# Gated cross-attention with a mixture of experts on one core: the turned selection goes to GpSimd, the low half of the second weights to VectorE, the additions take the high halves first, and the result is formed by bank and stored by tile

## The reference

```python
e = idx.reshape(-1)
onehot = jax.nn.one_hot(e, E, dtype=jnp.int32)
pos = jnp.sum(onehot * (jnp.cumsum(onehot, axis=0) - 1), axis=1)
valid = pos < CAP
buf = jnp.zeros((E, CAP, D), xt.dtype).at[e, posc].add(x_pairs)
g = jnp.einsum('ecd,eid->eci', buf, W1)
u = jnp.einsum('ecd,eid->eci', buf, W3)
h = jax.nn.silu(g) * u
out = jnp.einsum('eci,edi->ecd', h, W2)
y_pairs = out[e, posc] * (w.reshape(-1) * valid)[:, None]
...
x = x + jnp.tanh(g_ffn[0]) * (y + shared)
```

## Time and profile before

| what | value |
|---|---|
| median of 3 runs | 411.07 us (410.23 to 413.1) |
| span of the profiled execution, first to last instruction | 405.0 us |
| median of the runs less that span | 6.07 us |
| PE busy | 358.6 us, 89% |
| DVE busy | 303.5 us, 75% |
| ACT busy | 250.9 us, 62% |
| POOL busy | 124.1 us, 31% |
| the expert loop (start of the first pass's first weights to the last addition) | 333.6 to 399.7 us |

### The profile page before, as it was taken

One profiled execution on the slowest core, in us unless ns is written; L12 is line 12 of the kernel. 1 busy time (PEld: TensorE's weight loads), 2 busy tenths in 40 slices (PEclk: granted clock), 3 DMA queues, 4 the chain that ended last, 5 costly groups with the idle time before them and its releaser, 6 DMA issues.

```text
span 405.0 us, 14019 instructions
## 1 busy us (share of the span) xinstructions
PE 358.6 (89%) x5793; PEld 269.3 (67%) x5793; DVE 303.5 (75%) x656; ACT 250.9 (62%) x412; POOL 124.1 (31%) x116
## 2 busy tenths in 40 slices
PE   0896899999998998998999999998864699999993
PEld 0663468668677766855866776786643587888882
DVE  3888886775776676586577668668896877999993
ACT  3476477777686676776768666567721535666761
POOL 6151462132022122222203300001101054787870
PEclk9999699999999999999999999999985858999998
DMA  7869965565294186166336208544000009635001
GB/s 253 196 157 197 241 146 134 87 159 136 58 171 115 53 152 182 54 106 175 103 61 125 54 14 142 129 137 141 3 2 2 1 1 306 191 116 163 2 0 45
DMA packets 34512, 45.65 MB, mean 113 GB/s; under 512 B 3995, under 2 KB 30299, under 8 KB 34323
## 3 DMA queue, kind: packets, MB, share of 16 engines
q1 hardware_dynamic: 33395, 43.74, 44.5%
q0 software_dynamic: 640, 0.78, 0.9%
q10 hardware_dynamic: 416, 0.26, 0.3%
HBM read 25.08 MB, written 0.47 MB: 63 GB/s over the span
## 4 chain that ended last, share of the span: by engine, by line
PE 76%; DVE 13%; issue 5%; ACT 2%; POOL 2%; DMA 1%; DVEq 0%; ACTq 0%; POOLq 0%
PE PS L1035 35%; PE PS L1101 9%; PE PS L1078 8%; PE PS L1112 7%; PE PS L1363 4%; PE PS L1322 3%; DVE mx L794 2%; PE PS L1088 2%; PE PS L1346 2%; PE PS L1312 1%; DMA x_in<-x 1%; DVE KN L743 1%; PE PS L1279 1%; DVE st L697 1%; DVE mtop L798 1%
## 5 line engine op out<-in xcount | busy, mean ns | idle before, releaser
L794 DVE TENSOR_REDUCE mx<-PS 112x1 f32<-112x500 f32 (+1 forms) x128 | 114.3, 933 | 52.8 <-PE PS L1078 52.7
L501 ACT ACTIVATE PT_all<-PS 128x1344 f32<-128x1344 f32 x64 | 82.6, 1290 | 10.1 <-PE PS L1101 9.9
L1035 PE MATMUL PS<-cT,wkvT 128*128 128x500 f16 x288 | 71.5, 385 | 18.0 <-POOL slot_of L404 11.2
L1035 PE MATMUL PS<-wkvT,cT 128*125 128x256 f16 x576 | 73.2, 279 | 0.0
L1035 PEld LDWEIGHTS PS<-wkvT,cT 128*125 128x125 f16 x576 | 65.3, 139 | 5.3 <-issue 0.5
L395 POOL TENSOR_TENSOR cT<-c_in,cT 128x1000 f16<-128x1000 f32 x18 | 37.5, 2082 | 86.9 <-ACT cT L479 86.9
L1035 PEld LDWEIGHTS PS<-cT,wkvT 128*128 128x128 f16 x288 | 27.5, 99 | 50.8 <-POOL slot_of L404 11.2
L486 ACT ACTIVATE KN<-PS,col_in 128x500 f16<-128x500 f32 x48 | 32.5, 677 | 40.6 <-PE PS L1035 40.6
L1078 PE MATMUL PS<-arena,QC 96*112 96x500 f16 x192 | 52.4, 380 | 3.1 <-issue 2.8
L1101 PE MATMUL PS<-QC,arena 98*128 98x112 f16 x768 | 49.2, 214 | 3.0 <-ACT QC L521 2.9
L493 ACT ACTIVATE V<-PS 125x512 f32<-125x512 f32 x48 | 28.7, 598 | 30.6 <-PE PS L1035 30.6
(11 more groups left out here) (207 smaller groups left out, 463.8 us busy)
## 6 DMA issues: line engine op xcount, KB each, us to landing
arena<-KN SPq DMA_DIRECT2D x144, 125.0 KB, 3.6
c_in<-ctx SPq DMA_DIRECT2D x24, 500.0 KB, 4.5
cT<-W SPq DMA_DIRECT2D x11, 352.0 KB
c_in<-W SPq DMA_DIRECT2D x6, 352.0 KB
cT<-W SPq DMA_DIRECT2D x11, 176.0 KB
arena<-place_far SPq DMA_DIRECT2D x1, 1568.0 KB, 10.0
c_in<-W SPq DMA_DIRECT2D x6, 176.0 KB
PT_all<-L_xattn_wkv SPq DMA_DIRECT2D x1, 512.0 KB, 6.1
```

Source lines behind the costliest of these rows:

```text
L501: act.activation(PT_all[:, u % 4, :].rearrange("p (c k) -> p c k", c=CH), PS[:, 3:6, 0:4 * TP], ACT.Exp, scale=SCORE).then_inc(s["exp_done ...
L794: dve.tensor_reduce(mx[:, u % 2, k:k + 1], PS[0:TP, k:1 + k * (CH - 1), 0:CW], AX.XY, ALU.max).then_inc(s["red_done"], 1)
L1035: ins = mm(out_, w(a, h), x_(b, h), start=first and k == 0, stop=last and k == len(todo) - 1)
```

## The change

Four edits, all in the expert loop and behind it.

1. `turned_select` moves from VectorE to GpSimd. It is the same instruction, issued there in a plain loop over the experts. Its waits are the same: the transfer of the places for experts 0 and 2, and `added` for the buffer.
2. `w2_lo` moves from GpSimd to VectorE for the experts 1 to 16 (index 0, the shared expert, stays). On VectorE it is one instruction that scales and subtracts, straight from the loaded weights, so the scaling step goes. It stands where the turned selection stood.
3. `add` runs over the high half for all four tiles first, and waits for the low half only then. In the last `add` a semaphore is raised after the second and the fourth tile.
4. The result is formed bank by bank after that semaphore, and each tile is stored by a transfer of its own.

```diff
+            out_v = out.rearrange("b s d -> (b s) d").rearrange("(t p) d -> p t d", p=TP)
+            for t in range(TT):
+                sp.wait_ge(s["y_final"], t + 1)
+                sp.dma_start(out_v[:, t, :], y_out[:, t, :]).then_inc(s["stored"], 16)
+            sp.wait_ge(s["stored"], 16 * TT)
...
-            for j in range(1, E + 1):
-                need(gp, "w2l_done", j)
-                w2_lo(j)
+
+            def turned_select(e):
+
+                if e == 0:
+                    gp.wait_ge(s["place_in0"], 16)
+                elif e == 2:
+                    gp.wait_ge(s["place_in1"], 16)
+                need(gp, "added", e - 1)
+                gp.tensor_scalar(selT[e % 2], place_row[:, e, :], slot_of[:, 0:1], None, ALU.is_equal).then_inc(s["st_done"], 1)
+
+            for e in range(E):
+                turned_select(e)
...
+            def w2_lo(j):
+
+                need(dve, "w2h_done", j + 1)
+                need(dve, "w2l_done", j)
+                dve.scalar_tensor_tensor(w2T[j % 2][:, 1], w2_in[j % NW], FS, w2T[j % 2][:, 0], ALU.mult, ALU.subtract).then_inc(s["w2l_done"], 1)
...
-                turned_select(e)
                 if e + 1 < E:
+                    w2_lo(e + 2)
                     hidden_rows(e + 1)
...
             w13_lo(1)
+            w2_lo(1)
...
             def add(e):
 
-                need(pe, "yl_done", e + 1)
                 need(pe, "st_done", e + 1)
-                for t in range(TT):
-                    for a in range(2):
+                for a in range(2):
+                    need(pe, "yl_done" if a else "yh_done", e + 1)
+                    for t in range(TT):
                         last = mm(PS[0:TP, t // 2, (t % 2) * D:(t % 2 + 1) * D], selT[e % 2][:, t * TP:(t + 1) * TP], y16[:, a, :],
                                   start=False, stop=e == E - 1 and a == 1, skip_group_check=True)
-                last.then_inc(s["added"], 1)
+                        if e == E - 1 and a == 1 and t % 2 == 1:
+                            last.then_inc(s["bank_added"], 1)
+                if e < E - 1:
+                    last.then_inc(s["added"], 1)
```

More of the change, by code:

```diff
@@ L254, in program @@
             gu_ready tanh_done h_done ht_ready hh_done hl_done y_ready yh_done yl_done added
-            y_final stored""".split()
+            bank_added y_final stored""".split()
         s = {n: sem(n) for n in names}
@@ L355, in _ @@
                 load_weights(j)
-            sp.wait_ge(s["y_final"], 1)
-            sp.dma_start(out.rearrange("b s d -> (b s) d").rearrange("(t p) d -> p t d", p=TP), y_out[:]).then_inc(s["stored"], 16)
-            sp.wait_ge(s["stored"], 16)
+            out_v = out.rearrange("b s d -> (b s) d").rearrange("(t p) d -> p t d", p=TP)
[3 more added lines that the diff above has]
+            sp.wait_ge(s["stored"], 16 * TT)
         @block.gpsimd
@@ L442, in _ @@
                         context_lo(b + 2, c)
[L443 to L449, removed]
-            need(gp, "t_ready", SLOTS - NPAIR)
-            w2_lo(0)
+            need(gp, "t_ready", SLOTS - NPAIR)
+            gp.wait_ge(w_in[0], 32)
+            gp.tensor_scalar(w2_s, w2_in[0], FS, None, ALU.mult).then_inc(s["w2_scaled"], 1)
+            gp.wait_ge(s["w2_scaled"], 1)
+            gp.wait_ge(s["w2h_done"], 1)
+            gp.tensor_tensor(w2T[0][:, 1], w2_s, w2T[0][:, 0], ALU.subtract).then_inc(s["w2l_done"], 1)
             for k, part in enumerate(groups):
@@ L1019, in _ @@
             result_lo(E - 1)
-            need(dve, "added", E)
             for t in range(TT):
-                last = dve.scalar_tensor_tensor(y_out[:, t, :], PS[0:TP, t // 2, (t % 2) * D:(t % 2 + 1) * D], tgf[:, 0:1], x1[:, t, :],
-                                                ALU.mult, ALU.add)
-            last.then_inc(s["y_final"], 1)
+                need(dve, "bank_added", t // 2 + 1)
+                dve.scalar_tensor_tensor(y_out[:, t, :], PS[0:TP, t // 2, (t % 2) * D:(t % 2 + 1) * D], tgf[:, 0:1], x1[:, t, :],
+                                         ALU.mult, ALU.add).then_inc(s["y_final"], 1)
         @block.tensor
```

## The result

The changed kernel takes 407.05 us as the median of 17 runs, the kernel before 410.23 of 17 beside it; the ratio is 0.9892 with a 95% interval of 0.9861 to 0.9924. So the change makes the kernel about 1% faster. The likeliest case, "within 1%", is just missed by that ratio. The ratio leaves out, for each kernel, the runs more than 1.5% above its own fastest one, 6 of 17 of the changed kernel and 3 of 17 before, which lowers it: the ratio of the medians of all runs is 0.9922, that of their means 0.9911, both inside 1%.

A forecast was written before the change was run, and what follows sets the result against it. Pace set by a ring through GpSimd's subtraction and VectorE's held-up selection. Loop -2.0, start +0.4 and end -1.8 sum to -3.4: span 405.0 to 401.6, plus 6.07 gives 407.7 us; range 406.3 to 412.0.

The forecast's parts named there:

- The ring through GpSimd's subtraction: Expert loop before: PE's turn, ScalarE, GpSimd's subtraction, VectorE's held-up selection, hidden rows, next turn; 3.955 us a pass.
- A pass afterwards: Expert loop after the change: slowest of four rings, 3.80 us a pass, saving 2.0 us over 13 passes.
- The first-weights ring: Expert loop: PE's results, ScalarE's copy and high half, VectorE's low half, PE's next first weights; 3.79 us, untouched.
- The hold: Expert loop: GpSimd's one-input selection keeps VectorE off the shared port for 0.54 us after its start.
- The ring of selection and port: Expert loop: GpSimd's selection holds up VectorE's low half of the second weights by some 0.27; 3.74 us a pass.
- PE alone: Expert loop: PE's own work per pass, 3.94 less the 0.17 wait that the new addition order removes; 3.77 us.
- The start: Start of the loop: low half of second weights replaces the selection in the first pass; +0.4 us, ends 0 and +1.3.
- The end: After the loop: first result bank freed sooner and a smaller last transfer; -1.8 us, ends -0.6 and -2.1.
- The bank's 0.62: End of the kernel: two additions instead of eight free the first result bank, six fewer at 0.104 each; 0.62 us.
- The 6.07: Whole kernel: median of the runs, 411.07, lies 6.07 us above the profiled span; left unchanged in the forecast.
- GpSimd getting in first: Loop rival: GpSimd's selection beats VectorE's line 963 (margin 0.07), so the loop gains nothing; 409.7 us, chance 0.20.
- The forecast keeps 0.58: Whole kernel: chance left for the main forecast of 407.7 us after rivals of 0.20, 0.12 and 0.10.

The follow-up runs named there:

- e8: Changed kernel with selection back on VectorE, GpSimd quiet in the loop, and ScalarE making the first weights' high half before the result's; ratio 0.9894, pass 3.72 us.
- e5: Changed kernel with the turned selection back on VectorE, beside the low half of the second weights, GpSimd idle in the loop; ratio 0.988, pass 3.806 us.
- e6: Changed kernel with ScalarE making the high half of the first weights ahead of the result's; 407.22 us timed once, pass 3.79 us once settled.
- e10: The changed kernel, unchanged, timed once more in another set of runs; ratio 0.9894 against the kernel before.
- e7: Changed kernel with three selection buffers, GpSimd's selection released by the low half of the first weights; 403.06 us timed once, pass 3.807 us.
- e4: Changed kernel plus an unused two-input GpSimd subtraction ahead of each turned selection from expert 2 on; 405.77 us timed once, pass 4.08 us.

## Why the prediction was right, and where it was wrong

*What bounds the kernel.* Right. The ring through GpSimd's subtraction set the pace; with it cut a pass fell from 3.955 to 3.806, and with GpSimd idle and the selection on VectorE it fell by just as much. Full as both were in the earlier trace rows, neither was at the end of what it could do: e8 runs 3.72 a pass on the same engines. One reading was a little off: not every VectorE instruction starts 0.08 ahead of the end of the one before, since line 994 starts 0.04 behind it (363.87 after 363.83).

*A pass afterwards.* 3.80 predicted, 3.806 measured, -2.0 against -1.93 in 13 passes. The first-weights ring was said to be the slowest at 3.79: it is 3.806 when seen alone (e5). The sign named for it, PE waiting for line 866 in every pass, is listed as a wait in e5 and not in the changed kernel. The hold was said to be 0.54 and to bring line 978 to some 0.95: it is about 0.49 behind line 970, and line 978 takes 0.98. The ring of selection and port was put at 3.74 and is 3.79 (e6), so the pass rests on two rings and not on one. PE alone was put at 3.77 and is 3.72 or less (e8), which the sum didn't need. The order of the additions is worth 0.04 a pass.

*The start.* +0.4 predicted, +0.36 in the profile; but with the clock of e10 it is -0.92, so a single start is no measure of the edits, and the agreement is in part luck. By the table, the first two passes took 8.15 to 8.44 with the loop as before and 8.52 to 8.69 in the changed loops with the same 13.7 of low clock, which is the predicted cost; in the changed loops with 6.8 they took 7.01 to 7.16. The prediction had no term for the clock. Ahead of the loop, put at 0, it was -0.12 in this pair, and over all executions the two ranges overlap. The lines ahead of the loop lost their hold as said: lines 940 and 953 take 0.23 and 0.21, where line 933, the old 940, took 0.66 and line 946, the old 953, 0.67.

```profile
329.24 0.23 DVE L940 TENSOR_TENSOR r<-r,rank 112x64 f32<-112x64 f32 x1
...
330.91 0.21 DVE L953 TENSOR_TENSOR r<-r 112x64 f32<-112x64 f32 x1
```

*The end.* -1.8 predicted, -1.63 measured. The bank's 0.62 is 0.62. The smaller last transfer lands in the 2.0 that the line between 448 KB and 14 KB gave; its term was 1.2 and gave 1.02, the one term that was visibly mis-sized. What it left out is that the four issues queue on SP: put "0.4 apart under the remaining tiles", they take 1.78 for four, and the last starts 0.16 later behind its tile than the single one did.

*The time.* The 6.07 that the prediction keeps above the span is no fixed cost. The span was that of one execution and the median that of others; in every run with a span of its own on record, the time is 1.7 to 2.9 above it. As only the difference of -3.4 was added, this did no harm.

*The rivals.* GpSimd getting in first did not happen, and could not be made to happen by starting it 0.09 ahead. Of the two kinds tried, only the two-input one holds to its end. The Trainium skill, "SBUF — State Buffer", section "SBUF: two separate sides", gives the shared pair of ports to whichever of a GpSimd instruction and a VectorE instruction with two SBUF inputs starts first, for the whole instruction. For the two-input subtraction the trace agrees (line 984 ends 0.54 after it, 1.28 long). For the one-input selection it doesn't: line 978 ends at 362.70, 0.23 ahead of GpSimd's 362.93, and "starts" can't be read from the records, as e7 shows. Line 974, by which the prediction found the trace to agree, has only one tensor as input; the case of two inputs is the one in e4.

*The chances.* This is the step that failed: "The forecast keeps 0.58", with a sixth of it over the 1% line, and 0.70 within 1%. The forecast was -3.4 us, 0.83%, and lay 0.7 us from the line at 406.96. A comparison of this kernel can be off by more than that: the kernel before against itself came out 1.4 us off. With 1.4 taken as one standard deviation, 0.7 is half of one, and about a third of the forecast belonged on the far side rather than a sixth (an estimate). The prediction weighed the scatter of the kernel only as "some scatter" at the end of its range, and gave no term to the clock ahead of the loop, which alone moves the start by 1.3.

What the runs showed in its place: the sum was close in its parts, -3.2 by stages for -3.4 forecast, and -3.7 ± 1.0 by all runs of both kernels. The line lies inside that. The first comparison fell on its far side at 0.9892, and by all its runs on the near side at 0.9911, so as far as is known it is the scatter, and which runs enter the ratio, and not a wrong mechanism that put it there. Whether the clock adds something for the changed kernel is open.

## What to carry to other kernels

When two engines are both full, look for the single instruction that takes several times its floor, and for what else runs in just that time; taking the instruction that holds up another engine off GpSimd paid, and in e5 moving all of it onto the "full" engine cost nothing. With ScalarE's order changed as well (e8) the pass fell further. Before spending effort on a ring, work out the next one: here it lay 0.02 us below, and cutting either alone gave next to nothing. Where a change is worth little more than the scatter, add it up from stages of the trace between fixed points, and set the chances around a threshold by the distance to it against the spread of a kernel timed against itself.

## What the runs showed of the hardware

- GpSimd and VectorE get into each other's way by the kind of GpSimd's instruction: one input (448 columns, float16, 1.40 us by itself) held VectorE for about 0.5 us (an estimate from line 978, 0.98 for 0.68) and let it go on beside it; two inputs (the same columns, 0.79 from the end of line 976) held it to the end.
- While VectorE's line 970, with two inputs in SBUF, ran, GpSimd's recorded instruction made next to no headway: 1.90 in place of 1.40. A GpSimd record that started 0.09 us ahead of VectorE's lost (e7), one 0.03 ahead won.
- Four transfers of 112 KB to memory, issued as the tiles came, landed 1.86 to 2.07 us after issue, one of 448 KB 3.2; four issues took SP 1.78.
